# Macaron block on one Trainium2 core: a smaller reciprocal, shared semaphores for emptied PSUM banks, new planner numbers, and GpSimd doing the rotation of three batches

## The reference

```python
x = x + 0.5 * ffn(layernorm(x))      # silu(g)*u with 704 inner columns, ternary weights with scales
x = x + attention(layernorm(x))      # 16 heads of 16, rotary positions on q and k, causal mask, softmax, Wo
x = x + 0.5 * ffn(layernorm(x))      # the same weights
```

## Time and profile before

| quantity | value |
|---|---|
| median of 3 runs | 982.24 us (974.79 to 982.36) |
| profiled execution, its own time | 987.35 us |
| its span, first to last instruction | 985.6 us |
| mean granted TensorE clock | 0.908 of full |
| TensorE / DVE / ACT / GpSimd busy in the span | 87% / 69% / 57% / 39% |

### The profile page before, as it was taken

One profiled execution on the slowest core, in us unless ns is written; L12 is line 12 of the kernel. 1 busy time (PEld: TensorE's weight loads), 2 busy tenths in 40 slices (PEclk: granted clock), 3 DMA queues, 4 the chain that ended last, 5 costly groups with the idle time before them and its releaser, 6 DMA issues.

```text
span 985.6 us, 17031 instructions
## 1 busy us (share of the span) xinstructions
PE 861.6 (87%) x6064; PEld 545.0 (55%) x6064; DVE 682.0 (69%) x1257; ACT 563.2 (57%) x1102; POOL 386.1 (39%) x361
## 2 busy tenths in 40 slices
PE   5699999969988989988898998798978878899996
PEld 4477888745544445644444464344434334777785
DVE  5575675868988779877787878777786742655442
ACT  5555665437465656664665655465635686465652
POOL 6556776352432234333134143221121322565453
PEclk9799999979996989986897988788979898999999
DMA  9500333035553325245054233431830110000101
GB/s 320 227 1 1 123 102 97 2 68 155 156 168 86 77 98 137 76 138 145 31 144 103 103 103 136 107 79 37 269 101 34 45 34 23 26 28 22 44 23 43
DMA packets 52320, 91.44 MB, mean 93 GB/s; under 512 B 6028, under 2 KB 17676, under 8 KB 51724
## 3 DMA queue, kind: packets, MB, share of 16 engines
q1 hardware_dynamic: 52092, 90.27, 30.2%
q10 hardware_dynamic: 144, 0.07, 0.0%
HBM read 47.49 MB, written 42.73 MB: 92 GB/s over the span
## 4 chain that ended last, share of the span: by engine, by line
PE 60%; DVE 15%; ACT 14%; issue 5%; DMA 2%; POOL 2%; SPq 1%; DVEq 0%; POOLq 0%; ACTq 0%
PE psum L909 12%; PE psum L799 12%; PE psum L773 10%; PE psum L861 9%; PE psum L892 7%; PE psum L824 7%; DVE NP L1148 7%; ACT PT L1029 5%; DVE SC L1170 3%; ACT XN L958 3%; PE psum L871 2%; ACT G_f L977 2%; DMA SC<-od 1%; ACT HH_f L987 1%; ACT XH L965 1%
## 5 line engine op out<-in xcount | busy, mean ns | idle before, releaser
L1148 DVE TENSOR_REDUCE NP<-psum 128x1 f32<-128x512 f32 (+3 forms) x640 | 364.3, 628 | 104.0 <-PE psum L871 74.3
L1029 ACT ACTIVATE PT<-psum 128x512 f32<-128x512 f32 (+2 forms) x640 | 307.9, 568 | 180.6 <-PE psum L892 179.5
L861 PE MATMUL psum<-K,Q 48*128 48x512 f32 (+2 forms) x768 | 159.8, 441 | 41.8 <-DVE NP L1148 31.7
L892 PE MATMUL psum<-Q,K 50*128 50x512 f32 (+2 forms) x768 | 153.8, 443 | 33.1 <-ACT PT L1029 18.0
L909 PE MATMUL psum<-PT,V 128*32 128x512 f32 (+3 forms) x1536 | 170.3, 568 | 0.4 <-ACT PT L1029 0.4
L1252 POOL TENSOR_SCALAR_AFFINE_SELECT PT<-PT 128x512 f32<-128x512 f32 x128 | 80.8, 638 | 206.1 <-ACT PT L1029 205.8
L799 PE MATMUL psum<-XH,WGH_f 128*128 128x512 f32 x352 | 147.2, 418 | 15.4 <-issue 6.7
L861 PEld LDWEIGHTS psum<-K,Q 48*128 48x128 f32 x768 | 77.1, 204 | 125.8 <-DVE NP L1148 48.5
L799 PE MATMUL psum<-XL,WGH_f 128*128 128x512 f32 x352 | 141.0, 401 | 0.0
L1209 POOL TENSOR_TENSOR HL_f<-HF_f,HH_f 128x512 fp32r<-128x512 f32 x80 | 103.0, 1294 | 94.1 <-ACT HH_f L987 93.8
L892 PEld LDWEIGHTS psum<-Q,K 50*128 50x128 f32 x768 | 77.4, 210 | 80.1 <-ACT PT L1029 31.8
(11 more groups left out here) (81 smaller groups left out, 1087.2 us busy)
## 6 DMA issues: line engine op xcount, KB each, us to landing
zd<-ZH SPq DMA_DIRECT2D x32, 512.0 KB, 3.8
Q<-zd SPq DMA_DIRECT2D x64, 192.0 KB, 3.7
K<-zd SPq DMA_DIRECT2D x64, 192.0 KB, 4.5
zd<-ZL SPq DMA_DIRECT2D x16, 512.0 KB, 4.6
od<-OS SPq DMA_DIRECT2D x32, 256.0 KB, 2.8
OC<-od SPq DMA_DIRECT2D x32, 128.0 KB
SC<-od SPq DMA_DIRECT2D x32, 128.0 KB
out<-X SPq DMA_DIRECT2D x16, 256.0 KB, 2.1
```

The source lines that it names most:

```text
L861: ins = tn.matmul(dst, Q[k][r, p, t * P:(t + 1) * P], K[k][r, p, ch * 512:ch * 512 + w], start=(m == 0), stop=not diag)
L892: ins = tn.matmul(dst, K[k][r, p, j * P:(j + 1) * P], Q[k][r, p, 512 * c2 + base:512 * c2 + 512], start=True, stop=True)
L1029: sc.activation(dst, src, ACT.Exp, scale=0.25).then_inc(S["act_exp"], 1)
L1148: ve.tensor_reduce(out=acc, in_=src, axis=AX, op=ALU.max, negate=True).then_inc(S["dve_max"], 1)
```

## The change

- The reciprocal is taken before the sums are repeated. For every group and half (32 times) a new DMA `rs` reads the four rows of sums out of `od` as a tile SU of 128x16, DVE takes the reciprocal into RC, a new DMA `rw` writes it to a new DRAM buffer, and the second DMA of `oc` repeats it from there into SC. The 16 reciprocals of 128x512 are gone.
- Pieces that empty banks raise one semaphore per engine (`act_out`, `dve_out`), and `take` waits for the latest first, so that an earlier piece of the same engine needs no wait.
- The planner has other durations and delays, costs for switching between shapes of matmul, a cost for a wait on a second engine, a bonus (`URGE`) for score pieces while few banks are held by their kind, QUOTA 5 in place of 4 and WINDOW 60 in place of 40. All five orders are therefore new.
- `TURN_POOL = (1, 2, 3)`: batches 1 to 3 (12 of the 16 pieces) use the second path of the rotation.
- Small constants share tiles (layout only).

```diff
--- before.py
+++ after.py
-TURN_POOL = ()
+TURN_POOL = (1, 2, 3)
...
+EMPTIES = {"act_exp": "act_out", "act_o": "act_out", "act_v": "act_out", "act_nt": "act_out", "act_xh": "act_out", "act_qk": "act_out",
+           "act_silu": "act_out", "dve_max": "dve_out", "dve_rope": "dve_out", "dve_xl": "dve_out", "dve_h": "dve_out", "dve_t2": "dve_out",
+           "dve_xo": "dve_out"}
...
-LAG = {"PE": 165, "ACT": 130, "DVE": 90, "POOL": 80, "SP": 1900}
+LAG = {"PE": 200, "ACT": 190, "DVE": 150, "POOL": 120, "SP": 1900}
...
-                cost = item[0] + (0 if self.mode[item[2]] == mode[0] else MODE_PLACE)
+                kind = item[2][0]
+                cost = item[0] + (0 if self.mode[item[2]] == mode[0] else MODE_PLACE) - URGE.get(kind, (0,) * 9)[held.get(kind, 0)]
...
-                            ns += MODE_NS
+                            ns += MODE_NS[mode[0], self.mode[piece]]
                             mode[0] = self.mode[piece]
+                        ns += WAIT_NS * (len({engine[x] for x in self.emptied.get(piece, ())}) - 1 > 0)
...
-MODE_PLACE, MODE_NS, DMA_RATE, WINDOW = 2.0, 110, 250.0, 40.0
+MODE_PLACE, WAIT_NS, DMA_RATE, WINDOW = 1.0, 80, 200.0, 60.0
+MODE_NS = {("full", "half"): 190, ("col", "half"): 110, ("half", "full"): 30, ("half", "col"): 30, ("full", "col"): 60, ("col", "full"): 60}
 AHEAD = 4.0
-QUOTA = {"pe_s": 4, "pe_st": 4}
+
+URGE = {"pe_s": (12, 12, 12, 12, 4, 0, 0), "pe_st": (12, 12, 8, 8, 0, 0, 0)}
+QUOTA = {"pe_s": 5, "pe_st": 5}
...
-                add(key, mask + (2 if u == "a" else 1) * (wide * 0.443 + 12), "pe_s", *unit, after=[ld(gr, ch), ld(gr, c2), ("act_mk",)],
+                add(key, mask + (2 if u == "a" else 1) * (wide * 0.443 + 40), "pe_s", *unit, after=[ld(gr, ch), ld(gr, c2), ("act_mk",)],
...
-                    w = sum({0: 1000, 128: 780, 256: 590, 384: 460}[e_skip(c2, i)] for i in (j - 1, j)) - 150
+                    w = sum({0: 790, 128: 600, 256: 420, 384: 250}[e_skip(c2, i)] for i in (j - 1, j))
...
                 add(key + 2.5, 600, *turn_of("ow", gr, c2), after=[("act_o", gr, c2)] + ([turn_of("oc", *was)] if gr else []), size=2.6e5)
+                add(key + 2.6, 600, *turn_of("rs", gr, c2), after=[turn_of("ow", gr, c2)])
+                add(key + 2.6, 280, "dve_rc", gr, c2, after=[turn_of("rs", gr, c2)] + ([turn_of("rw", *was)] if gr else []))
+                add(key + 2.6, 600, *turn_of("rw", gr, c2), after=[("dve_rc", gr, c2)] + ([turn_of("oc", *was)] if gr else []))
                 free = [("pe_o", b - 1, 4 * c2 + i) for i in range(4)] if b else []
-                add(key + 2.5, 1200, *turn_of("oc", gr, c2), after=[turn_of("ow", gr, c2)] + free, size=2.6e5)
+                add(key + 2.6, 1200, *turn_of("oc", gr, c2), after=[turn_of("ow", gr, c2), turn_of("rw", gr, c2)] + free, size=2.6e5)
                 if g % 2:
                     gp = g // 2
-                    add(key + 6, dve_ns(512), "dve_rc", b, gp, c2, after=[turn_of("oc", gr - 1, c2), turn_of("oc", gr, c2)])
-                    add(key + 6, pool_ns(512), "pool_on", b, gp, c2, after=[("dve_rc", b, gp, c2)])
+                    add(key + 6, pool_ns(512), "pool_on", b, gp, c2, after=[turn_of("oc", gr - 1, c2), turn_of("oc", gr, c2)])
...
     def wait_ge(self, sem, *step):
         value = self.done[(sem,) + step]
+        sem = EMPTIES.get(sem, sem)
         if self.met.get(sem, 0) < value:
...
-                for was in emptied.get(piece, ()):
+                for was in sorted(emptied.get(piece, ()), key=lambda was: -done[was]):
                     e.wait_ge(*was)
...
                 elif kind == "dve_rc":
-                    b, gp, c2 = a
-                    for g in range(2):
-                        e.wait_ge(*turn_of("oc", NG * b + 2 * gp + g, c2))
-                    n = 2 * (2 * gp + c2)
-                    ve.reciprocal(OC[n + 1][:, :], OC[n + 1][:, :]).then_inc(S["dve_rc"], 1)
+                    gr, c2 = a
+                    e.wait_ge(*turn_of("rs", gr, c2))
+                    if gr:
+                        e.wait_ge(*turn_of("rw", gr - 1, c2))
+                    ve.reciprocal(RC[c2][:, :], SU[c2][:, :]).then_inc(S["dve_rc"], 1)
...
+                elif name[:2] == "rs":
+                    gr, c2 = a
+                    e.wait_ge(*turn_of("ow", gr, c2))
+                    if gr:
+                        e.wait_ge("dve_rc", gr - 1, c2)
+                    src = OD[c2].rearrange("(h r) q -> h r q", h=4)[:, HD, :].rearrange("h (a n) -> h a n", n=16)
+                    sy.dma_start(SU[c2][:, :], src).then_inc(sem, 16)
+                elif name[:2] == "rw":
+                    gr, c2 = a
+                    e.wait_ge("dve_rc", gr, c2)
+                    if gr:
+                        e.wait_ge(*turn_of("oc", gr - 1, c2))
+                    sy.dma_start(RD_[c2].rearrange("h (a n) -> h a n", n=16), RC[c2][:, :]).then_inc(sem, 16)
                 elif name[:2] == "oc":
                     gr, c2 = a
                     b, g = divmod(gr, NG)
                     e.wait_ge(*turn_of("ow", gr, c2))
+                    e.wait_ge(*turn_of("rw", gr, c2))
...
-                    sy.dma_start(sc_[r, :], src[:, HD:HD + 1, :].broadcast_to([4, HD, 512])).then_inc(sem, 16)
+                    sy.dma_start(sc_[r, :], RD_[c2].unsqueeze(1).broadcast_to([4, HD, 512])).then_inc(sem, 16)
```

More of the change, by code:

```diff
@@ L321, in x_pass @@
         add(at, 110, "dve_nb", who, c, after=[("pool_rs", who, c)])
-        add(at + 2, 4 * 290, "act_xn", who, c, after=[("dve_nb", who, c)] + ([("pe_xT",) + xn + (1,)] if xn else []))
+        add(at + 2, 4 * 491, "act_xn", who, c, after=[("dve_nb", who, c)] + ([("pe_xT",) + xn + (1,)] if xn else []))
         for kt in range(2):
-            add(at + 4, 436, "pe_xT", who, c, kt, after=[("act_xn", who, c), ("act_id",)] + (x_users(*x) if x else []), room=(1,))
+            add(at + 4, 400, "pe_xT", who, c, kt, after=[("act_xn", who, c), ("act_id",)] + (x_users(*x) if x else []), room=(1,))
             add(at + 5, act_ns(512), "act_xh", who, c, kt, after=[("pe_xT", who, c, kt)] + (x_users(*x) if x else []))
@@ L363, in ffn @@
             if i < NI - 1:
-                add(key, 908, "pe_g", ph, c, i, after=x_in(who, c) + w + room, room=(1,))
-            add(key + 1, 908, "pe_u", ph, c, i, after=x_in(who, c) + w + room, room=(1,))
+                add(key, 925, "pe_g", ph, c, i, after=x_in(who, c) + w + room, room=(1,))
+            add(key + 1, 925, "pe_u", ph, c, i, after=x_in(who, c) + w + room, room=(1,))
             gate = ("pe_g" if i < NI - 1 else "pe_u", ph, c, i)
-            add(key + 1, act_ns(512) + 90, "act_silu", ph, c, i, after=[gate] + ([("dve_h",) + g] if g else []) + first,
+            add(key + 1, 586, "act_silu", ph, c, i, after=[gate] + ([("dve_h",) + g] if g else []) + first,
                 empties=[gate] if i < NI - 1 else [])
@@ L370, in ffn @@
                 empties=[("pe_u", ph, c, i)])
-            add(key + 2, act_ns(512), "act_hh", ph, c, i, after=[("dve_h", ph, c, i)] + room)
+            add(key + 2, 550, "act_hh", ph, c, i, after=[("dve_h", ph, c, i)] + room)
             add(key + 3, pool_ns(512) if i < NI - 1 else dve_ns(512), *hl_by(ph, c, i), after=[("act_hh", ph, c, i)])
@@ L399, in qkv @@
             for ab in range(2):
-                add(key(2 * w + ab), 1362, "pe_qk", b, cc, w, ab, after=x_in("a", c) + [("act_wh", "q"), ("pool_wl", "q")] + ([("pool_zl",) + was] if was else split), room=(1,))
+                add(key(2 * w + ab), 1385, "pe_qk", b, cc, w, ab, after=x_in("a", c) + [("act_wh", "q"), ("pool_wl", "q")] + ([("pool_zl",) + was] if was else split), room=(1,))
             banks_of = [("pe_qk", b, cc, w, ab) for ab in range(2)]
@@ L471, in heads @@
             was = pt_before(gr, c2, j)
[L472 removed]
+            add(key, (2 if u == "a" else 1) * (max(512 - skip, 256) * 0.443 + 40), "pe_st", *unit,
                 after=([was] if was else ffn1_end) + [ld(gr, c2), ld(gr, j // 4), turn_of("nm", gr, c2), (f"dma_on{gr % QK}",)],
@@ L600, in macaron @@
         MB = place("MB", [P, P + 64], BF16)
-        NH = place("NH", [P, 4])
-        ONE = place("ONE", [P, 1])
+        CST = place("CST", [P, 8])
+        NH, ONE, FS = CST[:, 0:4], CST[:, 4:5], CST[0:1, 5:6]
         FL = place("FL", [P, 16])
-        FS = place("FS", [1, 1])
         FLAG = place("FLAG", [1, 2], I32)
-        ST, MV, VE, RS, NB = ([place(f"{n}{i}", [P, 4] + s) for i in range(2)]
-                              for n, s in (("ST", [6]), ("MV", [2]), ("VE", []), ("RS", []), ("NB", [])))
+        ST, MV = ([place(f"{n}{i}", [P, 4, s]) for i in range(2)] for n, s in (("ST", 6), ("MV", 2)))
+        ROW = place("ROW", [P, 2, 3, 4])
+        VE, RS, NB = ([ROW[:, i, n, :] for i in range(2)] for n in range(3))
         NP = [place(f"NP{i}", [P, 2, BT, 4]) for i in range(2)]
@@ L610, in macaron @@
         NMT = [place(f"NMT{i}", [32, P], F32R) for i in range(2)]
```

(17 more changed lines are left out.)

11 lines of the change are left out of this document (6 added, 5 removed).

## The result

The changed kernel takes 921.4 us in the median of 4 runs (918.2 to 927.5), beside 981.8 for the kernel before; the ratio is 0.941 with a 95% interval of 0.934 to 0.947 (it is worked out from the single executions and differs a little from that of the medians, 0.938). The forecast was 929 with a range of 890 to 968. The profiled execution took 918.21 us with a span of 916.5, so 69.1 us of span are gone. It is the fastest execution of the changed kernel, and the profiled one of the kernel before was slower than all four that stand beside it; between the medians 60 us are gone. Ahead of the reading one correction that the experiments force: the sum came out near by luck.

What follows compares the result with a forecast made beforehand. Attention was taken to be bound by three engines handing banks round, where a late DVE delays TensorE. Terms -28 - 5 + 2 + 8 - 5 - 13 - 12 = -53 took 982 to 929 us, range 890 to 968.

Steps and rivals of the forecast that it cites:

- What bounds the kernel: Attention: no engine is full; three engines hand eight banks round in fixed order, and a late DVE makes TensorE late.
- TensorE is bound anyway: Rival: in attention only the reciprocals on the chain go, gain -20, 962 us; chance 0.16.
- no change: Rival: the new order spends what DVE gives, with banks in other hands; 980 us, chance 0.08.
- Reciprocal, -28: DVE in attention: big reciprocals had 33 us on the chain, the small ones put 5 back; -28 us.
- The transfers: Added DMAs `rs` and `rw` before SC is filled: taken as 0, bounds -14 and +31 us.
- my own mark of 15 us of waiting for SU: Changed profile: the forecast is wrong if DVE waits for SU over 15 us in all.
- Rotation, +5 before its share of load and clock, -4 with it: Rotation moved to GpSimd: DVE chain -5, ACT copies +2, masks +8; its share of load and clock is 9 us.
- masks behind a longer block: GpSimd: masks stand behind a 7.7 us rotation block where there were 2.6; +8 us, bounds 0 and +48.
- Shared semaphores, -5: TensorE's queue: half of 640 score pieces lose a wait, 16 us of queue time; -5 us, bounds 0 and -16.
- Less load -13: DVE in attention: a shorter queue brings maxima sooner, their 65 chain us cut by a fifth; bounds 0 and -41.
- clock -12: Attention: fewer TensorE stalls raise the mean clock by 2.5 hundredths, 5 us each; bounds 0 and -60.
- The new orders, 0, bounds +30 and -32: Planner's new orders: nothing in the trace prices them; taken as 0, bounds from stalls and TensorE's idle time not due to DVE.

Runs made afterwards that it cites:

- 53.5 us of load: Changed kernel, orders unchanged, with 16 further VectorE instructions of about 3.2 us before small reciprocals, unknown to the planner: 978.2 us, ratio 0.996.
- three pairs with equal planner numbers: Rotation on GpSimd against VectorE: changed kernel 921.4 and 911.4; with scores due 4.3 ahead 938.6 and 925.9; with old planner numbers 969.5 and 946.0 us.
- without the products: Changed kernel, orders unchanged, with the four products of each GpSimd rotation replaced by tiny memsets: 921.0 us, ratio 0.938.
- the two nudged orders: Scores due 4.3 in place of 4.0 ahead, same work: changed kernel 938.6 us (0.957); changed kernel with all rotation on VectorE 925.9 us (0.947).

## Why the prediction came out right, and which steps did not

The parts can be laid on one path of measured kernels: small reciprocals and shared semaphores 1 to 0.968, planner numbers to 0.927, rotation on GpSimd back to 0.941. In us: -33, -35 (946.0 to 911.4), +10; by the ratios -31, -40, +13. Between kernels that differ in their order each step carries the 14 to 17 us that one nudge can move, so only the first two are larger than the draw.

- *What bounds the kernel.* Right. A delay on DVE is a delay of TensorE: in unchanged orders 53.5 us of load cost 57. The rivals "TensorE is bound anyway" and "no change" are out, by this and by the measured 921.4.
- *Reciprocal, -28.* Mechanism right, size about right: +30 when it is put back and planned for. The share of 0.62 taken from the chain is near the 0.55 by which a load that the order doesn't expect lengthened TensorE's idle time; what I had too small is the clock on top of it, which doubled the price to the load's full length. I did not see that the planner had this reciprocal at 598 ns. The kernel before paid for a length nobody had told it, and how much of the gain a right number alone would have brought is open. The transfers cost nothing that matters, as taken; my own mark of 15 us of waiting for SU was passed (25.0), but 20.7 of it lie behind the last maximum.
- *Rotation, +5 before its share of load and clock, -4 with it.* Wrong sign, as far as three pairs can say. It costs 10, 13 and 23 us in three pairs with equal planner numbers (13, 10 and 18 by the ratios). The place I gave it, masks behind a longer block, is refuted in the changed kernel's orders: without the products nothing changes. DVE's relief of 28 us in attention did not pay. The remaining differences are the 24 bank copies in ScalarE's stream, the time that TR is held, and what the planner makes of these and of the long block; no run here separates them, so the cause stays open. As three draws of an order could share a sign by chance, neither sign nor size is firm.
- *Shared semaphores, -5.* Count wrong (65 waits, not 320); the time, -10 with overlapping intervals, is not shown to differ from nothing.
- *Less load -13, clock -12.* The clock was under-sized: 6 hundredths and not 2.5, 30 us of busy time. My price of 5 us a hundredth fits the measured 30 us for 6. The reason I gave does not fit my own rows: TensorE does not stand much more in attention than in the feed-forwards. It was idle for 12.2% of attention, and for 13.1% (11 us of it before its first input was there) and 10.5% of the two feed-forwards, at clocks of 0.87, 0.98 and 0.99.
- *The new orders, 0, bounds +30 and -32.* This is the step that failed: they are worth -35 (rotation on VectorE) and -48 (rotation on GpSimd) with the small reciprocals, beyond the bound, and -16 to -18 on the kernel before. Against the two nudged orders it is -20 (946.0 to 925.9) and -31 (969.5 to 938.6), so that it is the draw that takes it past the bound; but all of these are far from 0. The bound took only TensorE's idle time that did not name DVE, as if an order could not shorten waits for DVE, and left out the clock that comes back with them.

That the sum of -53 stood is luck in good part. The missing 35 to 48 for the orders were booked in part under load and clock (-25): idle time and clock are what a better order saves too, and these runs cannot tell whose they are. The rest was taken back by a rotation that measured 14 us or more dearer than my -4.

## What to carry to other kernels

Where several engines hand a few buffers round in an order fixed beforehand, look first at what the planner believes of each instruction: here it had one at 598 ns that took 3346. A delay on VectorE that the order doesn't expect was paid here at its full length, half as waiting and half as clock, though VectorE was busy only 67% of the time; a load of the same length that the order knew cost 30 us and not 57, in an order that was another draw. Before crediting a change with 10 us in such a kernel, nudge the order without changing the work and see how far the time moves. The changed kernel is best taken without its rotation on GpSimd: 911 us.

## What the runs showed of the hardware

The busy time of the same matmuls varied from 831 to 862 us between orders, and its product with the mean granted clock stayed within 778 to 790.

How much TensorE stands does not by itself set the clock. In one and the same execution of the changed kernel it was busy 92% of attention at a clock of 0.93, and 91% of the second feed-forward at 0.99; in the kernel before it was busy 88% of attention at 0.87 and 90% of the second feed-forward at 0.99. Whether it is the place of the idle time or the kind of the matmuls that decides is not settled by these runs.

GpSimd can hold up DVE. In the kernel before the longest of the subtractions on the maxima (190 ns in the median) ran as long as the GpSimd instruction that had started just before it, and both ended within 0.1 us of each other:

```profile
419.08 2.32 DVE L1164 TENSOR_TENSOR NM<-NP,NM 128x16 fp32r<-128x16 f32 x1
```

```profile
419.00 2.36 POOL L1245 TENSOR_TENSOR ZL<-TR,ZH 128x1024 fp32r<-128x1024 f32 x1 [0.23 <-ACT ZH L994]
```

The longest of the casts beside them did the same: 1.30 us from 204.14 us, beside a GpSimd instruction of 1.30 us from 204.10.

This is not where the time goes. The three kinds of small DVE instructions on the maxima took 23.9 us in all before (10.1 + 9.9 + 3.9), 24.4 with 61 us more of GpSimd work (9.9 + 8.4 + 6.1), and 20.7 without the products (8.2 + 9.7 + 2.8). The page "SBUF — State Buffer" of the Trainium skill ("Who interferes with whom") says that a DVE instruction with two SBUF inputs contends with a GpSimd instruction that reads SBUF. The subtraction is such an instruction, and the trace agrees with its 2.32 us.
